# Batch 0's expert tiles and residual sum placed earlier, first expert weights spaced by a unit, splits of maxima last in a unit, key parts on GpSimd

## The reference

```python
x = layernorm(x + retention(x))                # 8 heads, q/k 64, v 128, rotary, decay, gate
x = layernorm(x + ffn0(x))                     # see below
x = layernorm(x + attention(x))                # 16 heads of 8, biases on q, k and v, no causal mask
x = layernorm(x + x @ ternary(weight))
# ffn0:
x = x + mla_attention(rmsnorm(x))              # 16 heads of 8, rope, causal, latent of 64 for k and v
x = x + moe(rmsnorm(x))                        # per token the one expert of 4 with the highest logit:
                                               # relu(x @ W1[e].T + b1[e]) @ W2[e].T + b2[e], 128 -> 512 -> 128
```

## Time and profile before

| | us |
|---|---|
| median of 3 runs | 1119.39 (1118.14 to 1120.41) |
| profiled execution, its own time | 1121.22 |
| its span | 1119.4 |
| PE busy | 933.4 (83%) |
| DVE busy | 808.5 (72%) |
| ACT busy | 657.1 (59%) |
| POOL busy | 348.7 (31%) |
| chain that ended last: PE, DVE, POOL, issue, ACT | 37%, 25%, 14%, 12%, 7% |

### The profile page before, as it was taken

How to read it: one execution, slowest core, us unless ns; L and a number is a source line. 1 busy time by engine, 2 the same in 40 slices (tenths; PEclk the granted TensorE clock), 3 DMA queues, 4 the chain that set the end, 5 groups by cost and what they waited for, 6 DMA issues and landing times.

```text
span 1119.4 us, 22895 instructions
## 1 busy us (share of the span) xinstructions
PE 933.4 (83%) x9022; PEld 480.6 (43%) x9022; DVE 808.5 (72%) x1309; ACT 657.1 (59%) x1347; POOL 348.7 (31%) x624
## 2 busy tenths in 40 slices
PE   5999999985765999989787757878998999999982
PEld 3777778774432443444273322224622223222231
DVE  3666667753858777776645539876697899999965
ACT  2555555453331776766545634856577788898950
POOL 2755566643142222222424301242331211211111
PEclk8999999996755999999799869999999999999995
DMA  7000000000050133201321141012303210000000
GB/s 268 1 2 1 1 1 2 1 1 7 9 173 17 35 121 120 55 19 40 95 83 31 34 148 35 21 40 76 95 21 121 63 34 19 19 19 2 5 20 19
DMA packets 49342, 52.52 MB, mean 47 GB/s; under 512 B 8810, under 2 KB 40554, under 8 KB 49076
## 3 DMA queue, kind: packets, MB, share of 16 engines
q1 hardware_dynamic: 44948, 48.12, 14.2%
q0 software_dynamic: 4288, 2.94, 1.0%
HBM read 32.37 MB, written 19.68 MB: 47 GB/s over the span
## 4 chain that ended last, share of the span: by engine, by line
PE 37%; DVE 25%; POOL 14%; issue 12%; ACT 7%; DMA 2%; another core or an unknown queue 1%; SPq 1%; POOLq 0%; DVEq 0%; ACTq 0%
DVE arena L1455 17%; PE banks L1220 11%; PE banks L1191 8%; PE banks L1160 5%; ACT arena L1358 4%; POOL arena L705 2%; PE banks L1295 2%; POOL arena L377 2%; PE banks L1303 2%; POOL arena L704 2%; POOL arena L380 1%; POOL arena L708 1%; POOL arena L689 1%; PE banks L1199 1%
## 5 line engine op out<-in xcount | busy, mean ns | idle before, releaser
L1358 ACT ACTIVATE arena<-banks 128x512 f32<-128x512 f32 (+3 forms) x896 | 444.8, 550 | 182.9 <-PE banks L1191 87.3
L1455 DVE TENSOR_REDUCE arena<-banks 128x2 f32<-128x1024 f32 (+1 forms) x448 | 476.1, 1106 | 94.4 <-PE banks L1167 44.0
L1220 PE MATMUL banks<-arena 128*32 128x256 f32 (+1 forms) x3328 | 270.0, 397 | 8.2 <-ACT arena L1371 5.9
L1160 PE MATMUL banks<-arena 56*128 56x512 bf16 (+3 forms) x896 | 170.5, 378 | 40.0 <-DVE arena L1455 27.7
L1191 PE MATMUL banks<-arena 61*128 61x512 bf16 (+4 forms) x896 | 170.3, 376 | 40.0 <-ACT arena L1358 35.8
L1061 POOL CAST arena<-arena 16x128 bf16<-16x128 f32 x32 | 9.0, 281 | 392.5 <-ACT arena L1387 382.5
L1191 PEld LDWEIGHTS banks<-arena 61*128 61x128 bf16 (+1 forms) x896 | 44.3, 93 | 201.8 <-ACT arena L1358 175.5
L1220 PEld LDWEIGHTS banks<-arena 128*32 128x32 f32 x3328 | 67.5, 110 | 138.0 <-issue 86.6
L1160 PEld LDWEIGHTS banks<-arena 56*128 56x128 bf16 x896 | 45.1, 97 | 64.5 <-DVE arena L1455 48.7
L603 DVE TENSOR_REDUCE arena<-arena 128x8 f32<-128x1024 f32 x16 | 19.5, 1220 | 60.6 <-ACT arena L731 60.6
L1071 POOL DMA_DIRECT2D arena<-arena x96 | 55.0, 576 | 10.9 <-POOL arena L1064 8.9
(11 more groups left out here) (218 smaller groups left out, 1386.7 us busy)
## 6 DMA issues: line engine op xcount, KB each, us to landing
arena<-k_products SPq DMA_DIRECT2D x32, 224.0 KB
arena<-q_products SPq DMA_DIRECT2D x64, 112.0 KB
q_products<-arena SPq DMA_DIRECT2D x16, 384.0 KB, 3.6
k_products<-arena SPq DMA_DIRECT2D x16, 384.0 KB, 3.5
arena<-e_w SPq DMA_DIRECT2D x22, 256.0 KB
arena<-arena POOLq DMA_DIRECT2D x96, 4.0 KB, 1.7
sorted_rows<-c_pads SPq DMA_DIRECT2D x2, 709.5 KB, 8.1
arena<-sorted_rows SPq DMA_DIRECT2D x2, 709.5 KB, 5.6
```

The costliest lines, as they stand in the source:

```text
L1160: ins = nc.tensor.matmul(bank(first + par)[:, 0:hi - lo], Qs[k_][rows, qc, x, qo:qo + P], Ks[k_][rows, x, lo:hi], start=True, stop=not (di ...
L1220: ins = nc.tensor.matmul(PS[h * VW:(h + 1) * VW, AV_BANK, o:end], V[:, b, kt, HG * g + h, :], Pr[u % PROBS][:, h, o:end], start=(kt == 0 a ...
L1358: s_.activation(Pr[s % PROBS][:, h, o:C], bank(q % SCORES)[:, o:C], ACT.Exp) \
L1455: v_.tensor_reduce(of, two_banks, AX.X, ALU.max).then_inc(ring_dve, 1)
```

## The change

- For batch 0, in steps relative to z = 55: the groups x go from 14, 15, 16 to 11, 11, 12, the tiles h and y from 15 to 17 to 12 to 14, the puts with them, the sum from 21 to 17, and all that is placed relative to it (stat, root, scale, D, q, k, their parts, v) four steps earlier. In absolute steps: x at 66, 66, 67, tiles at 67 to 69, puts at 68 to 70, sum at 72, D at 77 and 78, q and k at 78 and 79, last parts at 81 and 82, v at 82 and 83.
- For batch 1 the tiles keep their place (pace two, step 15), the sum and what follows it comes one step earlier (128 to 127).
- The first four weight loads of either batch wait for one unit more than before; the load of the sorted rows is issued ahead of the fourth instead of behind it.
- A block's split on POOL is an item of its own, "split", sorted behind all others of its step. PE's and ACT's part of "M" stay where they were.
- k_part0 and k_part1 of the second layer run on POOL as tensor copies instead of on ACT; the query parts stay on ACT.

```diff
--- before.py
+++ after.py
@@ -830,13 +830,13 @@
 
             z = first_unit(2 * NG * (b + 1)) + 1 + Y_LAG
             one, two = 2 * b, 2 * b + 1
-            pace, end = ((4, 21), (2, 25))[b]
+            pace, tile, end = ((4, 12, 17), (2, 15, 24))[b]
             at = [(-7, ("square", (b, 0))), (-6, ("square", (b, 1))), (0, ("square", (b, 2))), (1, ("square", (b, 3))),
                   (1, ("norm", b)), (4, ("H", (b, 0))), (4, ("H", (b, 1))), (5, ("G", b)),
                   (7, ("C", b)), (7, ("sort", b)), (8, ("steer", b)), (9, ("bias", b)), (9, ("base", b))]
-            at += [(14 + g * 4 // pace, ("x", (b, g))) for g in range(len(GROUPS))]
+            at += [(tile - 1 + max(0, 4 * g // pace - (pace == 4)), ("x", (b, g))) for g in range(len(GROUPS))]
             for i in range(SORTED + 1):
-                step = 15 + min(i, SORTED - 1) // pace
+                step = tile + min(i, SORTED - 1) // pace
                 at += [(step, ("h", (b, i)))] * (i < SORTED) + [(step, ("y", (b, i - 1)))] * (i > 0)
                 at += [(step + 1, ("put", (b, i - 1)))] * (i > 0)
             at += [(end, ("sum", b)), (end + 1, ("stat", (b, 0))), (end + 2, ("stat", (b, 1))), (end + 2, ("root", b))]
@@ -856,7 +856,7 @@
                 scans.setdefault(scanned(u), []).append(u)
             for m in range(MS):
                 end = first_unit(m + 1)
-                after.setdefault(scanned(end - 1) + 1, []).append(("M", m))
+                after.setdefault(scanned(end - 1) + 1, []).extend([("M", m), ("split", m)])
                 after.setdefault(end + 1 + O_LAG, []).append(("O", m))
                 if m // 2 % NG == NG - 1:
                     bc = (m // 2 // NG, m % 2)
@@ -880,7 +880,7 @@
                     seq += pairs[x * len(pairs) // 2:(x + 1) * len(pairs) // 2]
                     if 0 < s <= NU:
                         seq.append(("V", (s - 1, x)))
-                seq += sorted(after.get(s, []), key=lambda e: e[0] != "put")
+                seq += sorted(after.get(s, []), key=lambda e: (e[0] != "put") + (e[0] == "split"))
             return seq + [("L", 3), ("T", 3), ("R", 2), ("P", 3), ("R", 3)]
 
 
@@ -1004,9 +1004,10 @@
 
                     steer = load_steer(b)
                     for i in range(W1S):
+                        if i == W1S - 1:
+                            load_sorted(b)
                         sp.wait_ge(score_done, HG * (paced + i))
                         load_w1(b, i, steer)
-                    load_sorted(b)
                     for i in range(W1S, SORTED):
                         load_w1(b, i, steer)
 
@@ -1026,7 +1027,7 @@
                 load_all(5)
                 load_all(6)
                 load_all(7)
-                route(0, first_unit(10) + 3)
+                route(0, first_unit(10) + 4)
                 fetch_rows(0)
                 store_parts(1, 0)
                 load_all(8)
@@ -1035,7 +1036,7 @@
                 load_all(10)
                 taken(sp, "Y", (1, 1))
                 sp.dma_start(wout, d["a_wo"]).then_inc(load4, 16)
-                route(1, first_unit(17) + 8)
+                route(1, first_unit(17) + 9)
                 load_all(11)
                 fetch_rows(1)
                 store_parts(1, 1)
@@ -1052,7 +1053,7 @@
                 pool.wait_ge(load2, 160)
                 link(g_.tensor_copy(hn[:, :, P].bitcast(U32), token.bitcast(U32)))
                 for kind, k in order():
-                    if kind == "M":
+                    if kind == "split":
                         n, c = divmod(k, 2)
 
                         part = [nmp[k % 2][:, i, :] for i in range(PARTS)]
@@ -1110,6 +1111,13 @@
                         pool.wait_ge(x_statted, 2 * (k + 1))
                         link(g_.tensor_scalar(rstd[:, t], mv[:, t, 1], 1e-5, None, ALU.add))
                         root_of(g_, link, newt[:, 1, t], rstd[:, t], newt[:, 0, t]).then_inc(x_rooted, 1)
+                    elif kind == "k_part0":
+                        taken(pool, "k", k)
+                        stored_wait(pool, 1, 1, k)
+                        g_.tensor_copy(parts[1][k % 2][:, 0, :], kq[1][k % 2]).then_inc(pj["k_part0"], 1)
+                    elif kind == "k_part1":
+                        parted(pool, "k_rem", k)
+                        g_.tensor_copy(parts[1][k % 2][:, 1, :], rem[1][k % 2]).then_inc(pj["k_part1"], 1)
                     elif kind == "k_rem":
                         parted(pool, "k_part0", k)
                         if k >= 2:
@@ -1425,15 +1433,13 @@
                             parted(act, "q_rem", k - 2)
                         s_.activation(kq[0][k % 2], bank(ring_bank(r)), ACT.Identity, bias=bqs, scale=QSCALE) \
                           .then_inc(ring_act, 1)
-                    elif kind in ("k_part0", "q_part0"):
-                        w = "qk".index(kind[0])
-                        taken(act, kind[0], k)
-                        stored_wait(act, 1, w, k)
-                        s_.activation(parts[w][k % 2][:, 0, :], kq[w][k % 2], ACT.Copy).then_inc(pj[kind], 1)
-                    elif kind in ("k_part1", "q_part1"):
-                        w = "qk".index(kind[0])
-                        parted(act, kind[0] + "_rem", k)
-                        s_.activation(parts[w][k % 2][:, 1, :], rem[w][k % 2], ACT.Copy).then_inc(pj[kind], 1)
+                    elif kind == "q_part0":
+                        taken(act, "q", k)
+                        stored_wait(act, 1, 0, k)
+                        s_.activation(parts[0][k % 2][:, 0, :], kq[0][k % 2], ACT.Copy).then_inc(pj["q_part0"], 1)
+                    elif kind == "q_part1":
+                        parted(act, "q_rem", k)
+                        s_.activation(parts[0][k % 2][:, 1, :], rem[0][k % 2], ACT.Copy).then_inc(pj["q_part1"], 1)
 
             @block.vector
             def _(dve):
```

## The result

The changed kernel takes 1102.5 us (median of four, 1101.5 to 1105.0), the kernel before on the same chip 1119.1 us (1118.1 to 1120.4): a ratio of 0.9854, 95% interval 0.9834 to 0.9874. The profiled execution took 1104.95 us, span 1103.2, mean granted clock 0.921 (before 1121.22, 1119.4 and 0.913).

The account below looks back on a forecast made before the run. Bound taken: one serial path, expert tiles through sum and projections to the stack's load, at the layer handover. -8.0 - 3.6 + 4.0 + 0 - 2.0 + 0.5 = -9.1 us from 1119.39: 1110, own range 1106 to 1114, wider 1103 to 1117.

Parts of the forecast that it names:

- Part 2: Batch 0's expert tiles three units earlier: costs 4.0 us (1.8 to 8), 2.2 waiting for sorted rows, 1.8 low clock.
- Part 1, the stalls: Units 76 to 88: DVE's wait for the sum and PE's for ACT, 4.6 us, go; gain 3.6 (0 to 10).
- Part 4: Key parts on GpSimd: eight ACT copies, 5.0 us, counted at 40%, gain 2.0 (0 to 5.0); DVE contention costs 0.5.
- nothing for the clock that comes back: From unit 89 on, DVE's two scans a unit fill it, so PE's recovered clock was counted as no gain.
- Part 1, the stack: Unit 89: PE's 8.86 us wait for the q_products load shrinks to 0.9; gain 8.0 us (6.3 to 8.9).
- the clock at 1.00 there: Sign of being right: PE's granted clock at 1.00 at unit 89, with no wait over 3 us for q_products.
- Part 3: Weight loads later: the 5.36 and 6.07 us holes before 545 and 756 belong to the sort; 0 (-6 to +1).
- Part 4, the casts: Units 78 to 82: a GpSimd cast of 128x512 takes 1.0 us, so the key parts cause no cost.
- (a): Late sorted rows keep PE's clock low through the expert tiles; ends at +10 us, 1129, or 1124; chance 0.08.
- (b): Projections obstruct scans in units 78 to 83; 4 us of unit 89's wait stay; gain 5 us, 1114.5; chance 0.17.
- (c): Weight loads make the holes before 545 and 756; spacing them takes half of each, 5 to 6 us, 1104; chance 0.10.
- (d): Moved-up sum waits for its rows with DVE's queue; time found at unit 89 lost at unit 73; 1119; chance 0.10.

Follow-up runs that it names:

- parts_only: The kernel before with only the key's two bf16 parts moved from ACT to GpSimd: 1112.1 us where before took 1117.5, ratio 0.9953.
- split_parts: The kernel before with late split and key parts together, old places and old weights: 1107.0 us where before took 1117.5, ratio 0.9907.
- after_third: The changed kernel once more, unedited, on a chip where the kernel before took 1104.1 us: 1094.9 us, ratio 0.9915.
- u_weights: The changed kernel with the weight loads and the sorted rows at their old thresholds: 1095.1 us where before took 1102.9, ratio 0.9922.

## Why the prediction was wrong

The direction was right, the size was not: 9.1 us forecast, 16.6 measured. By its own steps:

**Part 2, the first step that failed: "Sum +4.0 us"**, with its lower bound at +1.8. Over units 66 to 76 the trace of the changed kernel is 0.4 us longer. The wait for the sorted rows came as forecast, 2.20 us for 2.2, and PE's idle time grew by as much, from 6.03 to 8.20 us. Wrong was the other half, +1.8 us for the clock: on the same 532 recorded multiplications PE is busy for 50.27 us before and 48.51 us after, 1.8 us less, with the clock at 0.92 and 0.95. A row at the low level did come behind the wait (0.65 from 552 to 556 us), but the kernel before had more of it. How much of that is the change's doing is open. Here is the same stretch of parts_only, whose list is that of the kernel before as far as unit 81:

```profile
546.67:600.53 53.86, 47.85 (x532) 32.26 (x530) 29.94 (x57) 25.94 (x68) 17.00 (x22) 0.97 0.26 78
```

Against it, with as much idle time as before and a clock of 0.97, the step costs 2.9 us, within its bounds. The step also looked only at what the move costs where the first tile lands, not at what it does to the last one: the puts, no longer piled up behind a split, lost their idle stretch (2.11 us on ACT, 1.74 on PE), in whose place PE has waits of up to 1.23 us. That stretch stood in the trace of before, with the four puts in front of it. On quiet chips, where there is no such stretch to lose and no stretch at the sort that covers the sorted rows' way, the step costs 8.4 us by the traces, just beyond its upper bound of 8.

**Part 1, the stalls, and Part 4, the second step that failed: sized too small.** 3.6 + 0.75 us were forecast for units 76 to 89; 5.7 came in the first pair and 9.9 on quiet chips. Split and key parts alone give 10.5 us, where the stalls (3.6) and the key parts (1.5 net) were 5.1. By these medians, of two stalling chips, they hold 5.4 of the 7.5 us that were missed; the places and the weight loads hold the rest, 6.1 us where 8.0 - 4.0 were forecast. The forecast counted four fifths of the two named stalls and 40% of the copies, and put PE's clock in these units at nothing without a reason: its "nothing for the clock that comes back" speaks of the stack's stretch. The clock alone is 4.6 us in split_parts. In the first pair it did not come: PE is busy for 38.73 and 38.54 us, at 0.87 and 0.88, and the 5.7 us are idle time (12.4 to 6.9 us). In after_third, the same kernel, the same work takes 34.69 us at 1.00. Why the clock stayed low in the one trace and not in the other is open.

**Part 1, the stack: right, a little small.** 8.0 forecast within 6.3 to 8.9; the wait of 8.86 us went altogether, and the stretch is 9.5 us shorter, of which PE's busy time is 0.2 (clock 0.76 and 0.81). On quiet chips the wait of before was 6.72 us and 6.7 went. DVE became the next limit as said: 24.32 of 25.63 us busy. The sign "the clock at 1.00 there" did not come: it was 0.59 from 648 to 652 us and 0.98 in the next 4 us.

**Part 3: right.** The stretches stayed, 5.19 and 4.90 us for 5.36 and 6.07. u_weights has 0.9922, where the changed kernel has 0.9915 and 0.9918: no difference, though on quiet chips, where there are no stretches. That the weights don't make them is read from the traces named above. The prediction tied the stretches to the sort, rightly, but did not see the reason, the distance of its transfers.

**Part 4, the casts: right in kind.** A GpSimd cast of 128x512 takes 0.61 us in six of eight cases and 1.07 in two, forecast 1.0. Contention was sized too low. Two lines of the changed kernel, minimum, median and maximum in ns:

```profile
L1120 POOL CAST arena<-arena x4: 613/843/1073, 623.6 to 836.0; 128x512 bf16<-128x512 f32 x4
```

```profile
L1580 DVE TENSOR_TENSOR arena<-arena x4: 683/1062/1549, 620.8 to 835.0; 128x512 f32<-128x512 f32 x4
```

DVE's four subtractions take 683 + 2 x 1062 + 1549 = 4.36 us instead of 4 x 0.69, 1.6 us more where 0.5 were taken; two of the four bear it, with 0.75 and 0.87 us. The Trainium skill's rule ("SBUF — State Buffer", "Who interferes with whom"), by which the later instruction waits for the whole of the other, is nearer to these rows than the prediction's 0.15 us a meeting. The meeting from which that figure was taken could not cost more: the GpSimd operations beside it are of 0.28 and 0.40 us. The contention did not show in the time: DVE was busy for 25.67 of 45.42 us in those units, and parts_only is 0.5% faster.

**The rivals.** (a) did not come: from 560 us on the changed kernel's windows show the clock at 1.00 through the tiles. (b) did not come: the last query part starts 16 us earlier and nothing of the stack's wait stays. (c) gave 1104, near the time, for a wrong reason: the sorts' stretches are about as they were. (d) did not come: DVE's statistics start without a wait.

**Luck.** On quiet chips the changed kernel gains 9.2 us (after_third), just the 9.1 of the forecast. That is errors that cancel: 8.4 us lost in units 66 to 76 where 4.0 were priced, 6.7 gained at the stack where 8.0 were, and 12.9 gained in units 76 to 89 and 132 to 146 where 5.1 were.

**The terms are not independent,** which a sum can't show. On stalling chips the places and the weight loads are worth 0.5% beside split and key parts (0.9907 to 0.9854, on two chips, the intervals just apart at 0.9879 and 0.9874); on quiet ones the places are worth nothing (0.9921 to 0.9918, on two chips), though alone they give 0.4%. What they take from the stack's wait is paid at the sorted rows.

## What to carry to other kernels

Price a moved step at both its ends: where it will wait, and what its end, piled up or spread, does to the others. A stall removed on a path where PE's clock is below 1.00 can give back PE's slower work as well (4.6 us in split_parts, 0.2 in the first pair): read its busy time for the same instructions from a stretch at 1.00 and put it into the range. A single trace of a kernel isn't enough for that: the same stretch differed by 2.4 us between two traces in which the program was the same (units 66 to 76, before and parts_only). And an idle stretch that ends at "<-remote" on several engines at once deserves a look at what GpSimd issues just before it.

## What the runs showed of the chip

Behind four indirect transfers that GpSimd issued some 1.3 us apart ACT stood idle for 2.1 us, DVE and PE for 1.6 to 1.7; beside eight of them ACT stood idle for 4.9 to 6.4 us, of which 1.2 to 1.4 us at the first sort stand on quiet chips as well, and SP's three issues took 7.1 us instead of 3.1. The traces show it on two chips, with before at 1117.5 and 1119.1 us. In two traces with the eight 1.86 us apart, on two more chips with before at 1116.1 and 1118.2 us, there was none. On three other chips (1102.9 to 1104.7 us) there was none at the close distance, and on the one of them where the wider was run none at that. The kernel before took 11 to 16 us less on these three. Whether this is a property of the chip or of the time at which it was met is not shown.
